# The products with the centroids in eight pieces of twelve, set between wide matmuls, in place of two lots of 48

## What is computed

```
xn   = layernorm(x)
attn = softmax(causal(xn qk xn^T / sqrt(128))) xn ov
aff  = xn @ centroids.T            # 8 experts
eid  = argmax(aff)                 # one expert for each token
h    = relu((layernorm(xn) * ln_g[eid] + ln_b[eid]) @ w1[eid] + b1[eid])
ffn  = xn + sigmoid(xn . centroids[eid]) * (h @ w2[eid] + b2[eid])
out  = x + attn + ffn
```

## Time and profile before

| | |
|---|---|
| median of three timed runs | 231.44 us |
| lowest and highest | 230.81 and 232.5 us |
| span of the profiled execution | 227.7 us |
| time of that execution with what lies around the span | not recorded by itself |
| PE busy | 210.9 us, 93% |
| mean granted clock of PE | 0.974 of full |

### The profile page before, as it was taken

One profiled execution on the slowest core, in us unless ns is written; L12 is line 12 of the kernel. 1 busy time (PEld: TensorE's weight loads), 2 busy tenths in 40 slices (PEclk: granted clock), 3 DMA queues, 4 the chain that ended last, 5 costly groups with the idle time before them and its releaser, 6 DMA issues.

```text
span 227.7 us, 6814 instructions
## 1 busy us (share of the span) xinstructions
PE 210.9 (93%) x2418; PEld 164.9 (72%) x2418; DVE 170.7 (75%) x441; ACT 151.2 (66%) x333; POOL 155.4 (68%) x224
## 2 busy tenths in 40 slices
...
PEclk9999999975899999999999999999999999999998
DMA  5991030899301111111111497556754111107575
GB/s 164 312 299 47 0 91 18 255 185 180 57 0 50 35 38 37 43 31 38 37 49 37 85 201 150 123 128 134 134 139 98 49 35 39 49 25 225 148 217 156
DMA packets 41345, 23.55 MB, mean 103 GB/s; under 512 B 12472, under 2 KB 39136, under 8 KB 41312
## 3 DMA queue, kind: packets, MB, share of 16 engines
...
...
...
## 4 chain that ended last, share of the span: by engine, by line
PE 73%; DVE 17%; issue 5%; DMA 2%; ACT 1%; ACTq 0%; DVEq 0%
PE psum L1324 9%; PE psum L1290 6%; PE psum L1291 6%; PE psum L1292 6%; PE psum L1267 5%; PE psum L1333 4%; PE psum L1422 4%; PE psum L1334 4%; PE psum L1450 4%; PE psum L1448 4%; PE psum L1449 4%; PE psum L1341 4%; PE psum L1424 4%; PE psum L1423 4%; DVE row_max L887 2%
## 5 line engine op out<-in xcount | busy, mean ns | idle before, releaser
L1042 ACT ACTIVATE p_sb<-psum 128x512 f32<-128x512 f32 (+1 forms) x80 | 41.8, 534 | 15.3 <-PE psum L1324 9.6
L1010 DVE SCALAR_TENSOR_TENSOR h_lo<-psum,h_hi 128x512 f16<-128x512 f32 x39 | 26.8, 690 | 25.1 <-ACT h_hi L1157 24.1
L685 POOL DMA_INDIRECT sorted_y<-xn x39 | 38.1, 976 | 10.8 <-issue 5.1
L1036 ACT ACTIVATE p_hi<-psum 128x512 f16<-128x512 f32 (+3 forms) x56 | 30.2, 542 | 20.2 <-PE psum L1341 13.0
L902 DVE TENSOR_TENSOR p_lo<-p_sb,p_hi 128x512 f16<-128x512 f32 (+3 forms) x56 | 33.4, 615 | 11.8 <-ACT p_sb L1042 10.7
L663 POOL MEMSET idle<- 1x600 f32 x71 | 41.7, 588 | 0.0
L676 POOL DMA_INDIRECT sorted_x<-xr,pos x32 | 34.4, 1076 | 9.3 <-issue 4.7
L1157 ACT ACTIVATE h_hi<-psum 128x512 f16<-128x512 f32 x39 | 23.3, 596 | 21.6 <-PE psum L1424 20.0
L887 DVE TENSOR_REDUCE row_max<-psum 128x1 f32<-128x512 f32 x48 | 31.7, 682 | 3.9 <-PE psum L1267 3.8
L1422 PE MATMUL psum<-v_full,w_hl 128*128 128x128 f16 x156 | 28.0, 219 | 0.6 <-issue 0.4
L1290 PE MATMUL psum<-qT_hi,kT_hi 128*128 128x512 f16 (+1 forms) x80 | 28.1, 352 | 0.3 <-ACT qT_hi L1135 0.3
...
## 6 DMA issues: line engine op xcount, KB each, us to landing
...
sorted_y<-xn POOLq DMA_INDIRECT x39
...
```

The source lines that it names most:

```text
L685: pool.indirect_dma_start(out=sorted_y[:, :], out_offset=bass.IndirectOffsetOnAxis(ap=tokens, axis=0), in_=xs[:, t % SLOTS, 0:P], in_offse ...
L1042: a.activation(p_sb[:, u, off:GW], bank[SCORE[n % R]][:, off:GW], ACT.Exp, scale=SCALE).then_inc(s_exp, 1)
```

## The change

Each AFF job is cut into four pieces of four tiles, twelve matmuls each: AFF.h is the first, AFFr.h.1 to AFFr.h.3 are the others. The bank is taken at the first piece, and the semaphore for DVE is counted at the last. Each piece waits for the keys of its own group only. For PE the list now reads: M.0.2.2.2, X.8, AFF.0, P.3, AFFr.0.1, M.0.3.1.0, AFFr.0.2, M.0.3.3.1, AFFr.0.3, M.0.3.2.0, AFF.1, P.4, AFFr.1.1, M.0.3.1.1, AFFr.1.2, P.5, AFFr.1.3, P.6, M.0.3.0.3, V.2, and so on as before. For DVE: RM.0.2, MR.0.3.1.0, MR.0.3.3.1, CH.0, MR.0.3.2.0, QT.0.0.1, MR.0.3.1.1, CH.1, MR.0.3.0.3, and so on. The ring then gives AFF.0 bank 6 and M.0.3.2.0 the same bank behind it, AFF.1 bank 7 and V.2 behind it; before, M.0.3.0.3 stood behind AFF.0 and M.0.3.3.2 behind AFF.1. From M.0.3.0.3 on, every job has the bank that it had. The rest of the list is as it was.

```diff
-... X.8 P.3 M.0.3.1.0 MR.0.3.1.0 M.0.3.3.1
-MR.0.3.3.1 M.0.3.2.0 MR.0.3.2.0 QT.0.0.1 AFF.0 M.0.3.1.1 MR.0.3.1.1 AFF.1 CH.0 CH.1 P.4 P.5 P.6 M.0.3.0.3 MR.0.3.0.3
+... X.8 AFF.0 P.3 AFFr.0.1 M.0.3.1.0 MR.0.3.1.0
+AFFr.0.2 M.0.3.3.1 MR.0.3.3.1 AFFr.0.3 M.0.3.2.0 CH.0 MR.0.3.2.0 QT.0.0.1 AFF.1 P.4 AFFr.1.1 M.0.3.1.1 MR.0.3.1.1
+AFFr.1.2 P.5 AFFr.1.3 CH.1 P.6 M.0.3.0.3 MR.0.3.0.3
...
-            def affinities(job):
-                h = job[1]
-                at = free_bank(job)
-                pe.wait_ge(s_fold, 2)
-                pe.wait_ge(s_klo, BG * (h + 1))
-                for t in range(BT):
+            def affinities(h, piece):
+
+                if piece == 0:
+                    free_bank(("AFF", h))
+                    pe.wait_ge(s_fold, 2)
+                at = bank[bank_of["AFF", h]]
+                pe.wait_ge(s_klo, h * BG + piece + 1)
+                for t in range(piece * GT, (piece + 1) * GT):
                     hi, lo = (k[:, (h * BT + t) * P:(h * BT + t + 1) * P] for k in (kT_hi, kT_lo))
                     to = at[:, t * E:(t + 1) * E]
                     mm(to, hi, cent_hi[:], start=True, stop=False)
                     mm(to, hi, cent_lo[:], start=False, stop=False)
                     m = mm(to, lo, cent_hi[:], start=False, stop=True)
-                m.then_inc(s_affp, 1)
+                if piece == BG - 1:
+                    m.then_inc(s_affp, 1)
...
                 if kind == "AFF":
-                    affinities(job)
+                    affinities(job[1], 0)
+                if kind == "AFFr":
+                    affinities(job[1], job[2])
```

More of the change, by code:

```diff
@@ L70 @@
 C0a C1a LE.1.2 C2a AE.0 Ta.0 AE.1 AE.2 AE.3 AE.4 W1h.0 W1h.1 Ta.1 LE.2.3 Vf.0 Qa.0 Qa.1 W1l.0 AE.5 LE.3.4 Va.0 Vf.1
[L71 to L79, removed]
@@ L80 @@
-Tl.3 Tl.4 Tl.5 QT.0.0.0 Tl.6 Tl.7 Q.3 X.7 Ql.3 M.0.2.2.2 MR.0.2.2.2 RM.0.2 X.8 P.3 M.0.3.1.0 MR.0.3.1.0 M.0.3.3.1
-MR.0.3.3.1 M.0.3.2.0 MR.0.3.2.0 QT.0.0.1 AFF.0 M.0.3.1.1 MR.0.3.1.1 AFF.1 CH.0 CH.1 P.4 P.5 P.6 M.0.3.0.3 MR.0.3.0.3
-V.2 X.9 X.10 M.0.3.3.2 MR.0.3.3.2 P.7 X.11 CNT SIG SH.0.2 M.0.3.3.3 PL Sl.0 MR.0.3.3.3 QT.0.1.0 QT.0.1.1 P.8 X.12 P.9
-P.10 P.11 M.0.3.0.1 MR.0.3.0.1 M.0.3.1.3 MR.0.3.1.3 X.13 X.14 X.15 X.16 X.17 P.12 M.0.3.2.2 MR.0.3.2.2 Sl.1 P.13 P.14
-M.0.3.2.3 MR.0.3.2.3 M.0.3.0.2 MR.0.3.0.2 M.0.3.1.2 MR.0.3.1.2 P.15 M.0.3.3.0 MR.0.3.3.0 X.18 M.0.3.0.0 MR.0.3.0.0
@@ L85 @@
[L85 to L124, removed]
@@ L125 @@
-SO.21 SO.22 SO.23 SO.24 SO.25 SO.26 SO.27 SO.28 SO.29 SO.30 SO.31 SO.32 SO.33 SO.34 SO.35 SO.36 SO.37 PB.68 P.69 PB.69
-P.70 X.73 PB.70 P.71 P.72 X.74 PB.71 X.75 X.76 PB.72 P.73 PB.73 P.74 PB.74 X.77 X.78 P.75 PB.75 P.76 PB.76 X.79 EH.77
-EX.77 EH.78 EX.78 P.77 PB.77 P.78 P.79 PB.78 EH.79 EX.79 QT.1.3.0 QT.1.3.1 SO.38 PB.79
+W1l.1 ROW.0.1 C1v C2v BIAS Tl.0 ROW.1.2 VAR.2.3 Tl.1 VAR.3.4 RN.4.8 BASE.3 W2l.0 W2l.1 BASE.4 BASE.5 BASE.6 COL0 BASE.7
+W2l.2 W2l.3 W2l.4 S.0 S.1 S.2 S.3 S.4 S.5 S.6 S.7 Ql.0 Ql.1 VAR.4.8 V.0 W1b.0 W1b.1 Q.0 Q.1 V.1 M.0.0.0.0 MR.0.0.0.0
@@ new lines @@
+M.0.0.1.0 MR.0.0.1.0 W1.2 W1.3 M.0.0.3.0 MR.0.0.3.0 W1b.2 W1b.3 M.0.0.2.0 MR.0.0.2.0 RM.0.0 T.2 M.0.1.1.0 MR.0.1.1.0
+Tl.2 W1.4 M.0.1.3.1 MR.0.1.3.1 M.0.1.0.1 MR.0.1.0.1 M.0.1.1.1 MR.0.1.1.1 XA.2 W1h.2 W1h.3 W1l.2 LE.4.8 Ta.2 W1l.3 W1l.4
+M.0.1.2.1 MR.0.1.2.1 Q.2 M.0.1.3.0 MR.0.1.3.0 Ql.2 M.0.1.2.0 MR.0.1.2.0 W1.5 ROW.4.8 SH.0.0 W1h.4 XA.3 Qa.2 XA.5
+SHa.0.0 W2.0 W2.1 W2.2 EX.0 W1h.5 EX.1 EX.2 XA.7 SHa.0.1 EX.3 W2.3 W2.4 R2a M.0.1.0.0 MR.0.1.0.0 RM.0.1 M.0.2.3.1
+MR.0.2.3.1 X.0 M.0.2.1.1 MR.0.2.1.1 M.0.2.2.0 MR.0.2.2.0 X.1 X.2 M.0.2.1.0 MR.0.2.1.0 M.0.2.2.1 MR.0.2.2.1 W1l.5 X.3
@@ new lines @@
+M.0.2.3.2 MR.0.2.3.2 SH.0.1 R2 Ta.3 Ta.4 Ta.5 EX.4 EX.5 Ta.6 Ta.7 Qa.3 P.0 M.0.2.0.1 M.0.2.1.2 MR.0.2.0.1 P.1
+MR.0.2.1.2 M.0.2.0.0 MR.0.2.0.0 X.4 X.5 M.0.2.0.2 MR.0.2.0.2 M.0.2.3.0 MR.0.2.3.0 R2n T.3 T.4 T.5 X.6 P.2 T.6 T.7 Tl.3
+Tl.4 Tl.5 QT.0.0.0 Tl.6 Tl.7 Q.3 X.7 Ql.3 M.0.2.2.2 MR.0.2.2.2 RM.0.2 X.8 AFF.0 P.3 AFFr.0.1 M.0.3.1.0 MR.0.3.1.0
+AFFr.0.2 M.0.3.3.1 MR.0.3.3.1 AFFr.0.3 M.0.3.2.0 CH.0 MR.0.3.2.0 QT.0.0.1 AFF.1 P.4 AFFr.1.1 M.0.3.1.1 MR.0.3.1.1
+AFFr.1.2 P.5 AFFr.1.3 CH.1 P.6 M.0.3.0.3 MR.0.3.0.3 V.2 X.9 X.10 M.0.3.3.2 MR.0.3.3.2 P.7 X.11 CNT SIG SH.0.2 M.0.3.3.3
@@ new lines @@
+PL Sl.0 MR.0.3.3.3 QT.0.1.0 QT.0.1.1 P.8 X.12 P.9 P.10 P.11 M.0.3.0.1 MR.0.3.0.1 M.0.3.1.3 MR.0.3.1.3 X.13 X.14 X.15
+X.16 X.17 P.12 M.0.3.2.2 MR.0.3.2.2 Sl.1 P.13 P.14 M.0.3.2.3 MR.0.3.2.3 M.0.3.0.2 MR.0.3.0.2 M.0.3.1.2 MR.0.3.1.2 P.15
+M.0.3.3.0 MR.0.3.3.0 X.18 M.0.3.0.0 MR.0.3.0.0 P.16 M.0.3.2.1 Sl.2 MR.0.3.2.1 V.3 V.4 V.5 X.19 V.6 V.7 X.20 P.17 Q.4
+P.18 P.19 W2.5 W2.6 PICK EX.6 EX.7 EX.8 EX.9 Vf.2 SGa Va.1 Sh.0 Va.2 SHa.0.2 EX.10 EX.11 EX.12 EX.13 EX.14 Sh.1 Sh.2
+Sh.3 Sh.4 Sh.5 EX.15 EX.16 EX.17 Va.3 Va.4 Va.5 Va.6 Va.7 EX.18 EX.19 EX.20 Qa.4 Sh.6 Sh.7 EX.21 EX.22 EX.23 SHa.0.3
@@ new lines @@
+EH.24 EX.24 Qa.5 Qa.6 EH.25 EX.25 EH.26 EX.26 EH.27 EX.27 EH.28 EX.28 EH.29 EX.29 SHa.1.0 AE.6 EH.30 EX.30 EH.31 AE.7
+EX.31 EH.32 EX.32 EH.33 EX.33 EH.34 EX.34 EH.35 EX.35 EH.36 EX.36 EH.37 EX.37 EH.38 EH.39 EX.38 EX.39 SHa.1.1 EH.40
+EX.40 EH.41 EX.41 EH.42 EX.42 W1h.6 EH.43 EX.43 EH.44 EX.44 EH.45 EX.45 EH.46 Qa.7 EX.46 Vl.1 Vl.2 Vl.3 Vl.4 Vl.5
+RM.0.3 Vl.6 Sl.3 Sl.4 BLK Sl.5 Vl.7 M.1.0.3.0 X.21 MR.1.0.3.0 Ql.4 X.22 REG X.23 SH.0.3 P.20 P.21 P.22 M.1.0.1.0
+MR.1.0.1.0 P.23 M.1.0.0.0 MR.1.0.0.0 X.24 QT.0.2.0 QT.0.2.1 M.1.0.2.0 MR.1.0.2.0 XL.24 Ql.5 Ql.6 SC.0 SC.1 SC.2 SC.3
@@ new lines @@
+SC.4 SC.5 SC.6 SC.7 SC.8 SC.9 SC.10 SC.11 SC.12 SC.13 SC.14 SC.15 SC.16 SC.17 SC.18 SC.19 SC.20 SC.21 SC.22 SC.23 SC.24
+SC.25 SC.26 SC.27 SC.28 SC.29 SC.30 SC.31 W2l.5 W2l.6 W2l.7 Q.5 Q.6 X.25 X.26 M.1.1.2.0 RM.1.0 XL.25 MR.1.1.2.0 X.27
+X.28 M.1.1.1.0 M.1.1.0.1 MR.1.1.1.0 MR.1.1.0.1 P.24 PB.24 P.25 M.1.1.3.1 MR.1.1.3.1 X.29 M.1.1.1.1 PB.25 XL.26 XL.27
+MR.1.1.1.1 M.1.1.3.0 MR.1.1.3.0 XL.28 Sl.6 P.26 PB.26 SH.1.0 P.27 PB.27 M.1.1.2.1 X.30 M.1.1.0.0 MR.1.1.0.0 XL.29
+MR.1.1.2.1 XL.30 P.28 P.29 M.1.2.2.1 RM.1.1 MR.1.2.2.1 X.31 PB.28 PB.29 X.32 X.33 P.30 PB.30 M.1.2.0.2 X.34 M.1.2.3.1
```

30 lines of the change are left out of this document (added).

## The result

The changed kernel takes 234.69 us in the median of four runs (233.35 to 237.01), the kernel before, run beside it, 231.59. The ratio is 1.020, with a 95% interval of 1.0115 to 1.029: slower by about 2%, where 228.2 us and 1.4% less were forecast. The profiled execution took 233.68 us, its span is 231.9 us.

What follows compares the result with a forecast made beforehand. PE was taken to bound the kernel, busy 93% of 227.7 us, with one slow-clock stretch. Saving 5.61 less 0.47 gives 5.14 us, less about 1.9 for the clock 3.25, off 231.44: 228.2 us, range 226.2 to 231.4.

Steps and rivals of the forecast that it cites:

- Nothing breaks the work from 47.90 on: PE after M.0.3.2.0's wait: unbroken work, so the clock is back at 52.0 to 54.0 us.
- The hole on AFF.0's bank: PE before M.0.3.2.0: waits for CH.0's second operation, 46.57 to 47.90, 1.33 us against 0.86 before, adding 0.47.
- rival D: Slower: the 1.33 us hole brings the clock's fall forward and narrow pieces keep it low; 231.9 to 232.4 us, chance 0.07.
- The price of a narrow product: AFF products on PE: 25.4 ns each, 0.305 us per piece of twelve, 2.44 us in all wherever they stand.
- The clock: PE's granted clock still falls near 48.6 us but returns after 3.4 to 5.4 us, costing 1.25 to 2.25 us.
- 5.61 us "lost" in the slow stretch: PE from 49.11 to 59.22: 10.11 us against 4.50 at full clock, 1.15 lost in the pause and 4.46 to the clock.
- rival A: The clock holds: gain 5.14 us, or 4.0 with the pause, so 226.3 to 227.4 us; chance 0.25.
- The pause of 1.15 us: PE in P.5, given to no engine: taken as gone after the change; if it stays, 1.15 us less gain.
- the likelier case: The pause in P.5 on PE is gone after the change, at 0.6.
- Sends by POOL: Row sends from 66.59 us on move with PE, no loss taken; up to 0.5 us may go where the halves join.
- The base: Whole kernel: median 231.44 us is 3.7 us above the 227.7 us span, taken as unchanging; gains come off the median.

Runs made afterwards that it cites:

- e6: The kernel before with only QT.0.0.1 moved behind CH.0 on DVE, no pieces and no bank moved; ratio 1.0159 to the kernel before.
- e3: The changed kernel with only QT.0.0.1 moved ahead of CH.0 on DVE; ratio 1.0047 to the kernel before.
- e1: The kernel before, unchanged, run again for a second profile; ratio 1.0016 to the kernel before.
- e4: The changed kernel's code in the order of before, four pieces of twelve one behind the other where the lots of 48 stood; ratio 0.9989 to the kernel before.
- e9: The kernel before, unchanged, once more on another chip; ratio 1.006 to the kernel before.
- e12: The kernel before reordered, lots of 48 whole: AFF.0 after P.3, AFF.1 before P.6, on DVE QT.0.0.1, MR.0.3.1.0, then CH.0; ratio 0.990 to the kernel before.
- e2: The changed kernel, unchanged, run again; ratio 1.018 to the kernel before.

## Why the prediction was wrong

- **The step that failed** is "Nothing breaks the work from 47.90 on". By its own sums QT.0.0.1 starts at 49.7 us and, 0.8 us long, is over at 50.5, with MR.0.3.1.1 behind it at 51.0; it used this only for the time of CH.1. It never asked who waits for QT.0.0.1. P.4 does: it could have begun at 48.44, and started at 51.31, when QT.0.0.1 had ended at 51.26. So the prediction had 2 us of this wait in its own numbers, at a price of nothing; the 0.7 us that line 815 took too long are the rest. e6 and e3 show it from both sides: the late query row alone costs 1.6%, and taking it away leaves 0.5%.
- **The hole on AFF.0's bank** was right: M.0.3.2.0 forecast for 47.90 and measured at 47.91, 1.1 us of wait by the profile's count. It isn't the mechanism of rival D, though D's 232.4 us came nearest: in e3 this hole was longer, 1.96 us from the end of streaming, and the clock was low for no longer than in e1. By the rule of the Trainium skill that the prediction cited ("TensorE: Matmul & The Clock Gate", section "A second HAM failure mode: psum-queue depth-cycling"), short halts at PSUM banks make the clock fall. Both waits of the change are such halts, for the ring's bank and for the sums in banks 3 and 4, but the one that the prediction had in mind went with 3.4 us of low clock (e3, 1.96 us of hole), and the other with 6.8 (e6, where it stands alone).
- **The price of a narrow product** was right: in the profile after the first piece starts at 44.71 and P.3 behind it at 45.02, 0.31 us for twelve, and e4's eight pieces cost nothing more than the two lots (1.22 and 1.20 us).
- **The clock** was mis-sized. The prediction took from one profile 6.1 us between the start of unbroken work and the clock's return. In e1 it was back 3.4 us after the fall, in the profile after 4.8 us after P.4 began. The 5.61 us "lost" in the slow stretch were those of one execution: in others the same order lost 3.9 less (e1, e9) or nothing (the order of before in e4). So the 5.14 us of rival A were probably not there to be won in most runs: on the chip of e1 the runs of before with a mean granted clock between 0.985 and 0.997 have the same median as those above (225.5 and 225.7 us), and only those at 0.985 or less take 227.8.
- **The pause of 1.15 us** is gone in the profile after, as the likelier case had it, but not by the change. It is absent in e1, e4 and e9, which have the old order, and one of 0.84 us stands in e12 with its whole lots. In the first profile of before the clock was low three times as long as in e1; whether the pause did that is only argued. That a fetch of instructions is behind it is not shown either.
- **Sends by POOL**: right. The first began at 66.85 us, 0.26 later than the earlier trace rows, and from P.7 to HI.0 the lag grew by 0.15 us, inside the 0.5 us that the prediction allowed.
- **The base.** The prediction put 3.7 us around the span. In all 13 profiles whose execution was timed it is 1.7 to 1.8 us. So the first profile of before belongs to a run of about 229.5 us, not of 231.44, and its experts' layers were of the short kind (57.7 us). The medians of the first runs were probably of the long kind; this is argued, not shown.

The 4.04 us that the first two profiles differ by after HI.0 are not the change's: e2 runs the same program with the short kind of layers, and within each set of runs the kind was the same for every kernel, before included. On which chips the first two profiles were taken isn't recorded, so that they differ by the chip is argued. That the 4 us came out close to what the wait costs in the timed runs is chance.
